# Raw tokens multiplied by centred weights, with a turned copy of the input in memory, in a three-layer attention and routing kernel

## The reference

```python
def layernorm(x):  # (x - mean) / sqrt(var + 1e-5), over the 512 features
    ...
def ffn(x, w_router, w_block):            # x: (8, 1024, 512)
    scores = einsum('bld,d->bl', x, w_router)
    _, top_idx = top_k(scores, 768)       # three quarters of the tokens of a sequence
    processed = gelu(einsum('bkd,de->bke', selected, w_block))
    return x.at[batch_idx, top_idx].set(processed)
x = x + 0.5 * ffn(layernorm(x), ...)
x = x + attention(layernorm(x), ...)      # Wq, latent K and V, softmax, v_up, Wout
x = x + 0.5 * ffn(layernorm(x), ...)
```

## Time and profile before

| | us |
|---|---|
| runs (3), median | 2382.53 |
| lowest, highest | 2381.05, 2382.56 |
| the profiled execution | 2386.42 |
| its span, first to last instruction | 2384.7 |
| PE busy | 2201.2 (92%) |
| DVE busy | 1805.1 (76%) |
| ACT busy | 1176.3 (49%) |
| POOL busy | 404.6 (17%) |
| mean granted TensorE clock | 0.975 |

### The profile page before, as it was taken

One profiled execution on the slowest core, in us unless ns is written; L12 is line 12 of the kernel. 1 busy time (PEld: TensorE's weight loads), 2 busy tenths in 40 slices (PEclk: granted clock), 3 DMA queues, 4 the chain that ended last, 5 costly groups with the idle time before them and its releaser, 6 DMA issues.

```text
span 2384.7 us, 53143 instructions
## 1 busy us (share of the span) xinstructions
PE 2201.2 (92%) x21504; PEld 1338.9 (56%) x21504; DVE 1805.1 (76%) x5077; ACT 1176.3 (49%) x2070; POOL 404.6 (17%) x510
## 2 busy tenths in 40 slices
PE   5789999999999999999998999989998999999997
PEld 4544477445674456744566446754466544765455
DVE  7668767887669877788777886788767888678747
ACT  4245643556435564345644565345643557435552
POOL 2001111212102121021210212111111111121131
PEclk9889999999999999999999999999999999999999
DMA  3200021200302002020020201211021110212000
GB/s 137 106 2 2 2 83 60 72 2 2 106 36 72 3 19 89 37 72 3 19 89 36 73 2 40 68 54 55 2 71 36 70 40 2 71 36 72 2 2 36
DMA packets 69633, 106.42 MB, mean 45 GB/s; under 512 B 2576, under 2 KB 32784, under 8 KB 67344
## 3 DMA queue, kind: packets, MB, share of 16 engines
q1 hardware_dynamic: 69392, 103.03, 12.6%
HBM read 64.75 MB, written 37.75 MB: 43 GB/s over the span
## 4 chain that ended last, share of the span: by engine, by line
PE 75%; DVE 13%; ACT 6%; issue 5%; POOL 1%; DMA 0%; DVEq 0%; POOLq 0%; ACTq 0%
PE psum L829 29%; PE psum L842 17%; PE psum L950 10%; PE psum L957 9%; PE psum L845 5%; ACT pr L809 3%; DVE part L1093 3%; PE psum L871 2%; PE psum L856 2%; DVE psum L1095 2%; DVE junk L1043 1%; DVE nt_l L1018 1%; DVE junk L1028 1%; DVE junk L1045 1%; ACT nt_h L723 1%
## 5 line engine op out<-in xcount | busy, mean ns | idle before, releaser
L809 ACT ACTIVATE pr<-psum 128x512 f32<-128x512 f32 x1152 | 617.7, 597 | 537.8 <-PE psum L845 537.7
L842 PE MATMUL psum<-qk,qk 32*128 32x512 f32 (+3 forms) x4608 | 516.7, 371 | 63.6 <-DVE part L1093 26.9
L1095 DVE CUSTOM_DVE_ANT_0 psum<-psum,mask_b 128x512 f32<-128x512 f32 (+3 forms) x1024 | 473.1, 522 | 106.1 <-PE psum L856 104.7
L842 PEld LDWEIGHTS psum<-qk,qk 32*128 32x128 f32 x4608 | 318.6, 187 | 386.3 <-ACT pr L809 313.9
L856 PE MATMUL psum<-qk,qk 32*128 32x512 f32 (+3 forms) x4608 | 513.1, 371 | 20.6 <-DVE part L1093 19.1
L1093 DVE TENSOR_REDUCE part<-psum 128x1 f32<-128x512 f32 x512 | 325.4, 682 | 58.5 <-PE psum L856 56.5
L856 PEld LDWEIGHTS psum<-qk,qk 32*128 32x128 f32 x4608 | 312.0, 187 | 45.5 <-DVE part L1093 22.8
L950 PE MATMUL psum<-pr,v_sb 128*32 128x512 f32 (+3 forms) x3072 | 314.3, 504 | 1.6 <-ACT ht L723 1.6
L957 PE MATMUL psum<-pr,ones 128*32 128x512 f32 (+3 forms) x3072 | 308.8, 496 | 0.0
L715 POOL TENSOR_SCALAR_AFFINE_SELECT pr<-pr 128x512 f32<-128x512 f32 x256 | 161.6, 650 | 835.2 <-ACT pr L809 835.2
L744 ACT ACTIVATE norm<-x,nmr,rstd 128x512 f32<-128x512 f32 x192 | 153.3, 816 | 163.0 <-DVE nmr L1012 163.0
(11 more groups left out here) (109 smaller groups left out, 3239.1 us busy)
## 6 DMA issues: line engine op xcount, KB each, us to landing
x<-x_dram SPq DMA_DIRECT2D x16, 1024.0 KB, 7.1
spill_x<-x SPq DMA_DIRECT2D x16, 1024.0 KB, 4.8
x<-spill_x SPq DMA_DIRECT2D x16, 1024.0 KB, 7.2
out_dram<-x SPq DMA_DIRECT2D x14, 1024.0 KB, 5.1
w_h<-scratch_o SPq DMA_DIRECT2D x28, 256.0 KB, 3.1
w_l<-scratch_o SPq DMA_DIRECT2D x28, 256.0 KB, 3.3
w_h<-scratch_q SPq DMA_DIRECT2D x6, 1024.0 KB, 4.9
w_l<-scratch_q SPq DMA_DIRECT2D x6, 1024.0 KB, 6.9
```

The costliest lines, as they stand in the source:

```text
L809: nc.scalar.activation(pr_of(b, g, u)[:, 2 * p + place, :], bank(e, place), ACT.Exp, scale=SCALE).then_inc(exp_ready, 1)
L842: eng.matmul(o, (k_h, k_h, k_l)[t][own, P * j:P * (j + 1)], (q_h, q_l, q_h)[t][own, queries], start=(t == 0 and at == 0), stop=False, skip ...
L1095: m = nc.vector.tensor_tensor_reduce(scores, scores, mask_b[:, BANK - w:BANK], 1.0, FAR, ALU.add, ALU.max, top_of)
```

## The change

Routed layers multiply the raw token by a weight from which each column's mean over the 512 inputs is taken, and scale behind the product: ((x - mean) * rstd) @ W = rstd * (x @ (W - column means of W)). The scale is given to the gelu's ACTIVATE as a per-partition operand.

- `WC` (new, once, in the opening): four float32 matmuls of ones by `raw_b` give the column sums, four DVE steps subtract them from `raw_b`. `WS` 0 waits for it.
- Layernorm 0: `NO` and `T` are gone. A second input, `x_turned`, holds x with features on partitions. `XQ` (new) loads it in two DMAs of 1 MB for a sequence, from SP's queue, at the head of group 2 of the sequence before, into the place of `nt_l`. `XH` (new, eight for a sequence, every second chunk of group 2): ACT copies to `nt_h`, POOL subtracts in place to `nt_l`.
- Layernorm 2: `NO` is gone; `T` turns x itself as soon as `O` has been added. ACT's and DVE's parts of `T` stay. Layernorm 1 keeps `NO` and `T`.
- The order of `opening`, `back` and `closing` is rewritten around this. In `opening` WC, four XH and WS 0 stand ahead of the statistics, and the DMAs are ordered turned half, w_block, x, x, router weights, turned half, other weights.
- `G` waits for `rstd`; `GX` no longer waits for `NO`, and in layer 1 for `T` instead.

```diff
     def opening():
-        out = []
+        out = [("WC", 0)] + sum([raw(0, i) for i in range(TC)], []) + [("WS", 0)]
         for c in range(NC):
             for i in range(TC * c, TC * (c + 1)):
                 out += stats(0, 0, i)
             out += scales(0, 0, c)
-        out += [("NO", 0, 0, 0), ("NO", 0, 0, 1)]
-        for i in range(NT):
-            out += [("T", 0, 0, i)] + ([("NO", 0, 0, i + 2)] if i + 2 < NT else []) + dot(0, 0, i)
-            out += [("WS", 0)] if i == TC else [("SC", 0, 0, 0)] if i == 5 else []
-        out += [("SC", 0, 0, 1)]
         for i in range(TC):
-            out += layer(0, 0, i) + [("RT", 0, 0, 2 * i), ("RT", 0, 0, 2 * i + 1)]
-            out += [("WS", 1), ("WS", 2), ("WS", 3)] if i == 1 else []
-        out += [("RF", 0, 0)] + [("GX", 0, 0, i) for i in range(NT)]
-        out += layer(0, 0, 4) + layer(0, 0, 5) + summed(0, 0) + summed(0, 1)
-        out += layer(0, 0, 6) + summed(0, 2) + summed(0, 3) + scales(1, 0, 0) + [("WS", 4)] + layer(0, 0, 7)
+        out += sum([raw(0, i) for i in range(TC, NT)], [])
+            out += dot(0, 0, i)
+        out += layer(0, 0, 0) + layer(0, 0, 1)
+        for i in range(TC, NT):
+            out += dot(0, 0, i)
+        out += [("SC", 0, 0, 0)] + layer(0, 0, 2) + [("SC", 0, 0, 1)] + [("RT", 0, 0, i) for i in range(3)] + [("WS", 1)]
+        out += [("RT", 0, 0, i) for i in range(3, 6)] + layer(0, 0, 3) + [("WS", 2)] + [("RT", 0, 0, 6), ("RT", 0, 0, 7)]
+        out += [("RF", 0, 0)] + [("GX", 0, 0, i) for i in range(NT)] + [("WS", 3)] + layer(0, 0, 4) + layer(0, 0, 5)
+        out += layer(0, 0, 6) + layer(0, 0, 7)
+        out += summed(0, 0) + summed(0, 1) + summed(0, 2) + summed(0, 3) + scales(1, 0, 0) + [("WS", 4)]
...
     def back(b):
-            return [("T", 2, b, i)] + ([("NO", 2, b, i + 2)] if i + 2 < NT else [])
+            return [("T", 2, b, i)]
-        out = added(0) + added(1) + more(maxima, 5) + added(2) + added(3) + scales(2, b, 0)
-        out += added(4) + [("NO", 2, b, 0), ("NO", 2, b, 1)] + more(maxima, 6) + added(5) + turn(0)
-        out += added(6) + more(gathered, 1) + turn(1) + added(7) + more(gathered, 0) + more(turned, 1)
-        out += [("VA", 2, b, 1), ("RS", 2, b, 1)] + turn(2)[:1] + dot(1, b, 0) + [("NM", 2, b, 1)] + more(turned, 0)
+        out = added(0) + added(1) + turn(0) + more(maxima, 5) + added(2) + turn(1) + added(3) + turn(2)
+        out += scales(2, b, 0) + added(4) + turn(3) + more(maxima, 6) + added(5) + turn(4) + dot(1, b, 0)
+        out += added(6) + turn(5) + more(gathered, 1) + dot(1, b, 1) + added(7) + turn(6) + more(gathered, 0) + more(turned, 1)
         out += ([("W2", b + 2, "q", 0)] if b + 2 < B else [])
-        out += layer(1, b, 0) + turn(3)[:1] + [("NO", 2, b, 4), ("NO", 2, b, 5)] + dot(1, b, 1) + dot(1, b, 2)
-        out += layer(1, b, 1) + turn(4) + dot(1, b, 3) + turn(5) + dot(1, b, 4) + turn(6) + [("SC", 1, b, 0)] + turn(7) + dot(1, b, 5)
-        out += layer(1, b, 2) + dot(1, b, 6) + dot(1, b, 7) + layer(1, b, 3) + [("SC", 1, b, 1)]
+        out += scales(2, b, 1) + layer(1, b, 0) + turn(7) + more(turned, 0) + dot(1, b, 2) + dot(1, b, 3) + dot(1, b, 4)
+        out += layer(1, b, 1) + [("SC", 1, b, 0)] + dot(1, b, 5) + dot(1, b, 6)
+        out += layer(1, b, 2) + dot(1, b, 7) + layer(1, b, 3) + [("SC", 1, b, 1)]
...
     def closing(b, left):
-        for i in range(TC, NT):
-            out += added(i)
-        out += scales(2, b, 1) + [("NO", 2, b, 4), ("NO", 2, b, 5)] + added(0) + added(1) + turn(4)
-        out += added(2) + turn(5) + dot(1, b, 4) + added(3) + turn(6) + dot(1, b, 5) + scales(2, b, 0) + turn(7) + dot(1, b, 6)
-        out += dot(1, b, 7) + [("NO", 2, b, 0), ("NO", 2, b, 1)] + layer(1, b, 4) + [("SC", 1, b, 1)]
-        out += dot(1, b, 0) + dot(1, b, 1) + dot(1, b, 2) + dot(1, b, 3) + turn(0)
-        out += turn(1) + layer(1, b, 5) + [("SC", 1, b, 0)] + turn(2) + turn(3)
+        out += added(4) + added(5) + turn(4) + added(6) + turn(5) + added(7) + turn(6) + scales(2, b, 1) + added(0) + turn(7)
+        out += dot(1, b, 4) + added(1) + turn(0) + dot(1, b, 5) + added(2) + turn(1) + dot(1, b, 6) + dot(1, b, 7)
+        out += added(3) + turn(2) + scales(2, b, 0) + [("SC", 1, b, 1)] + dot(1, b, 0) + dot(1, b, 1) + dot(1, b, 2)
+        out += dot(1, b, 3) + layer(1, b, 4) + turn(3) + [("SC", 1, b, 0)] + layer(1, b, 5)
...
-            groups[2] += [[("NO", 0, b + 1, 0), ("NO", 0, b + 1, 1)]]
+            groups[2][0] += [("XQ", b + 1, c) for c in range(NC)]
+            for i in range(NT):
+                groups[2][2 * i + 2] += raw(b + 1, i)
             chunks = groups[3]
-            for u in range(NT):
-                chunks[2 * u] += [("T", 0, b + 1, u)]
-                chunks[2 * u + 1] += [("NO", 0, b + 1, u + 2)] if u + 2 < NT else []
...
+                elif k == "XQ":          # SP
+                    b, c = e[1:]
+                    if b:
+                        sp.wait_ge(s_done, nth["S", b - 1, 1, UNITS - 1, 1])
+                    eng.dma_start(nt_raw[(b + 2) % 3][:, TC * c:TC * (c + 1), :, :], x_turned[b, :, TC * c:TC * (c + 1), :, :]
+                                  ).then_inc(xt_in[c], 16)
...
+                elif k == "XH":          # POOL
+                    pool.wait_ge(xh_ready, nth[e])
+                    nc.gpsimd.tensor_tensor(nt_l[n][:, i, :, :], nt_raw[n][:, i, :, :], nt_h[n][:, i, :, :].bitcast(F32),
+                                            ALU.subtract).then_inc(xl_ready, 1)
...
+                elif k == "XH":          # ACT
+                    act.wait_ge(xt_in[i // TC], 16 * (b + 1))
+                    copy(nt_h[n][:, i, :, :], nt_raw[n][:, i, :, :]).then_inc(xh_ready, 1)
...
+                    act.wait_ge(rstd_ready, nth["RS", 2 * f, b, i // TC])
-                         ACT.Gelu_apprx_tanh).then_inc(gelu_ready, 1)
+                         ACT.Gelu_apprx_tanh, scale=rstd[:, 2 * f, i:i + 1]).then_inc(gelu_ready, 1)
...
+                if k == "WC":            # PE
+                    pe.wait_ge(raw_in[0], 16)
+                    for n in range(NK):
+                        m = eng.matmul(bank(e), ones[:, 0:1].broadcast_to([P, P]), raw_b[:, n, :], start=(n == 0), stop=(n == NK - 1))
+                    m.then_inc(wc_done, 1)
...
+                if k == "WC":            # DVE
+                    dve.wait_ge(wc_done, 1)
+                    for n in range(NK):
+                        nc.vector.scalar_tensor_tensor(out=raw_b[:, n, :], in0=bank(e), scalar=-1.0 / E, in1=raw_b[:, n, :],
+                                                       op0=ALU.mult, op1=ALU.add).then_inc(centered, 1)
```

More of the change, by code:

```diff
@@ L289, in ending @@
         return out
-    sched = [("XL", 0, 0), ("XL", 0, 1)] + opening()
+    sched = [("XQ", 0, 0), ("XL", 0, 0), ("XL", 0, 1), ("XQ", 0, 1)] + opening()
     for b in range(B):
@@ L335, in program_order, with macaron @@
     return sched, beside
-def macaron(nc, x, w_q, w_lat, w_qk, w_vu, w_out, w_router, w_block, scratch_q, scratch_o, spill_x, out):
+def macaron(nc, x, x_turned, w_q, w_lat, w_qk, w_vu, w_out, w_router, w_block, scratch_q, scratch_o, spill_x, out):
     sched, beside = program_order()
@@ L352, in macaron @@
             load_nth[e] = 1 + sum(1 for o in load_nth if o[2] == e[2])
+    norms = [e for e in sched if e[0] == "NO"]
     steps = [e[1:4] for e in sched if e[0] == "S" and e[4] == 0]
@@ L410, in macaron @@
             continue
-        if k == "XT" and e[2] > 0 or k in ("T", "SC", "F") and e[1] == 0 and e[2] > 0 and (k != "F" or e[3] < 2):
+        if k == "XT" and e[2] > 0 or k in ("SC", "F") and e[1] == 0 and e[2] > 0 and (k != "F" or e[3] < 2):
             banks[e] = from_queue(1)
@@ L474, in macaron @@
         nt_l = [over(f"nt{n}_l", region[n] + 16384, [P, NT, NK, P], F32R) for n in range(3)]
+        nt_raw = [over(f"nt{n}_raw", region[n] + 16384, [P, NT, NK, P]) for n in range(3)]
         nt_act = [over(f"nt{n}_act", region[n], [P, NT, NK, P]) for n in range(3)]
@@ L523, in macaron @@
         t_done, th_ready, tl_ready = sem("t_done"), sem("th_ready"), sem("tl_ready")
+        xt_in, xh_ready, xl_ready = [sem(f"xt_in{c}") for c in range(NC)], sem("xh_ready"), sem("xl_ready")
+        wc_done, centered = sem("wc_done"), sem("centered")
         sc_done, srow_ready, scol_ready = sem("sc_done"), sem("srow_ready"), sem("scol_ready")
@@ L865, in _ @@
                     pe.wait_ge(*freed(*user))
-                if k == "T":
-                    s, b, i = e[1:]
-                    pe.wait_ge(no_ready, nth["NO", s, b, i])
-                    slot = nth["NO", s, b, i] % 2
+                if k == "WC":
[3 more added lines that the diff above has]
+                    m.then_inc(wc_done, 1)
+                elif k == "T":
+                    s, b, i = e[1:]
+                    if s == 1:
+                        pe.wait_ge(no_ready, nth["NO", s, b, i])
+                        tile = norm[:, nth["NO", s, b, i] % 2, :]
+                    else:
```

(9 more changed lines are left out.)

28 lines of the change are left out of this document (22 added, 6 removed).

## The result

The changed kernel takes 2327.53 us (median of 4 runs, 2326.72 to 2328.94) against 2382.55 us (4 runs, 2381.05 to 2382.6): 55.0 us less, ratio 0.977, 95% interval 0.9756 to 0.9784. The forecast was 2328, so what has to be examined is whether the terms are right or only their sum.

A forecast was written before the change was run, and what follows sets the result against it. PE was taken as the bound (92% busy, 97% in group 3), DVE's chain at both ends. Terms -42 + 3.5 - 17 - 6.6 + 8 = -54 us took 2382.5 to 2328 us, range 2311 to 2352.

The forecast's parts named there:

- Group 3, -6.0 us a sequence: Group 3, seven times: layernorm 0's eight transposes and waits for `scol` go, 6.0 us a sequence, -42 us in all.
- The unknown: Group 3: whether PE closes the gaps around a removed T; 0.5 us for a T if not, 0.69 us expected.
- Group 2, +0.5 us a sequence: Group 2, seven times: ACT's copies and POOL's subtractions added there cost 0.5 us a sequence, +3.5 in all.
- rival 4: Groups 0 and 3 and opening: other waits shorten too, opening loses only 4 us; 2312 us, chance 0.10.
- The load is hidden by about 4 us: Group 2: turned loads land 4.9 us after issue, wanted 9 us after; cost 0, each us beyond stops ACT one.
- `back`, -2.4 us: `back`, seven times: PE's waits for DVE go as T no longer waits for `norm`; -2.4 us each, -17 in all.
- Gelu with a scale, 0: Gelu on ACT, 128 times: the scale operand adds 0 to 0.22 us each, hidden; cost 0 on the path.
- The closing, -6.6 us: Closing: a shorter chain from last add lets the ranks begin at about 2350.1 instead of 2356.73 us; -6.6 us.
- The opening, +8 us: Opening: weight preparation ahead of the statistics delays the first CB by 7 us, plus 1 for contention; +8 us.
- The term for contention: Opening: DVE's dots beside POOL's last four subtractions are slowed, 1 us added.
- the estimate of 3 us: Opening: by the skill's shared SBUF interface rule, dots beside POOL are delayed, costing some 3 us instead of 1.
- rival 1: `back`: new waits replace the old, PE waits as much as before, only -37 is left; 2345 us, chance 0.15.

The follow-up runs named there:

- run 3: Changed kernel plus 32 unread transposes a sequence on TensorE in group 3, in two blocks of 16, sequences 0 to 6: 2349.84 us, +22.3 us against the changed kernel.
- Run 1: Changed kernel with layernorm 0 of sequences 1 to 7 taken back to normalized, transposed tokens: 2372.54 us, +45.0 us against the changed kernel.
- run 5: Changed kernel with the turned loads of sequences 1 to 7 issued about 9.6 us later: 2382.71 us, +55.2 us against the changed kernel.
- run 2: Changed kernel with layernorm 2 taken back, old `back` and `closing`, second gelu without scale: 2346.3 us, +18.8 us against the changed kernel.
- run 7: Changed kernel with the splits of tiles 4 to 7 of sequence 0 put ahead of the opening's statistics: 2326.25 us.
- run 8: Changed kernel with the opening's statistics ahead of the column sums' subtraction and its dots right behind that: 2321.63 us, -5.9 us against the changed kernel.

## Why the prediction was right

1. **Group 3, -6.0 us a sequence.** Right, and by its own mechanism: the loop takes 23.57 us (23.5 forecast), and each four transposes put back alone cost 0.68 us (0.69 forecast). In the traces the stretch from first to last `S` gives 6.36 us a sequence: 5.5 for eight T, as forecast, and 0.87 for the waits, of which the forecast took 0.5. The unknown, whether neighbours would close up below 0.5 us, is answered by run 3: only if the transposes stood in one block would four cost 0.44.
2. **Group 2, +0.5 us a sequence.** Mis-sized, near the lower bound: the trace shows 0.1 us. Run 1 gives 45.0 us where 42 - 3.5 = 38.5 was the forecast for groups 2 and 3 together. Of the difference of 6.5 us this term has 2.6 and the waits of group 3 have 2.6. Groups 0 and 1 were not in the sum: they are 4.6 us shorter in seven sequences (3.7 with group 2), which is the direction of rival 4; by which wait isn't shown.
3. **The load is hidden by about 4 us.** Right: ACT never waits for it in group 2. The first `XH` needs only the first of the two loads, and in all seven sequences that one lands 4.9 to 5.1 us after issue (4.9 forecast), so some 4 us of the 9 are left. The second lands later and is wanted later. The price outside the cover was too mildly put. The forecast had one us lost for one us late; run 5 shows 7.9 us for a stop of 6. By that the change is worth nothing once ACT's stop reaches 6 us instead of 7.7, that is with a landing 15 us after issue instead of 17.
4. **`back`, -2.4 us.** 2.0 measured in `back` 3, 2.2 as the mean of seven stretches of `project` and `back`: the `scol` wait grew from 0.3 to 0.7, since the dots were not quite done in time.
5. **Gelu with a scale, 0.** Right: 0.69 us for each instead of 0.60, and no wait behind it. The Trainium skill's 93 ns for a pointer operand (ScalarE: Activation LUTs, section "What ACT_TABLE_LOAD costs") agrees: 688 less 598 ns is 90.
6. **The closing, -6.6 us.** From last add to ranks it is 7.1 us, but that is not what the closing gains. The forecast left the last add where it was and so put nothing for the four more `T` ahead of it on PE; they make it 2.3 us later. 4.8 us are gained by the trace, from the first add to the ranks as from the last `S` to the end. With `back`, 15.1 + 4.8 = 19.9 us; run 2 shows 18.8 at the median, 23.6 was forecast.
7. **The opening, +8 us.** The end is right, +8.9 us at the first `S` and +8.8 by subtraction, but the way there isn't. The first CB is 10.7 us later, not 7 and one for contention, and 1.8 of it are made up before the first `S`. The term for contention was 1 us and measured 3.9 (1.05 for `nmr`, 1.07, 0.87 and 0.87 for three dots). Here the rule of the Trainium skill that was set against it (GPSIMD Engine Reference, section "Key points") was the better guide: the estimate of 3 us made by it lies nearer to 3.9 than 1 does. How much of the 3.9 us reaches the end no run shows: run 7 had the dots at full speed, but its statistics began 2.3 us later.

The sum with what was measured: -45.0 - 18.8 + 8.8 = -55.0, where the last term is by subtraction and the sum therefore comes out in any case; forecast -38.5 - 23.6 + 8 = -54. The check on it is the table: it has +8.9 for that term without any subtraction. The mechanisms of the forecast hold, but that it came within 1 us is in part luck: a gain taken 6.5 us too small stood against one taken 4.8 us too large. Rival 4 had that direction for groups 0 to 3, rival 1 the opposite one for `back`; neither is large enough to have decided.

## What to carry to other kernels

Where an engine is 96% busy, the price of an operation there is best read as the difference between two instances of the same loop, one with it and one without; a block of the same instructions alone is cheaper (0.44 against 0.69 us here) and misleads. What replaces it goes where the other engines have slack by the window, and the place matters more than the amount: the same eight splits cost 0.1 us a sequence in one group and 5.3 in the next. Ends of a kernel have their own bound: list what the chain there needs first, put only that first, and price each added preparation against it (a better order of the same work brought the first `S` 10.4 us forward here). Where an operation moves ahead of another, the other moves back: price both, as the closing shows.

## What the runs showed of the hardware

- **VectorE beside GpSimd.** Beside POOL's 128x512 subtraction of two SBUF tiles, DVE steps with two SBUF operands went from 0.75 to between 1.57 and 1.82 us for 128x512, and even one of 128x4 elements from 0.16 to 1.21 us, so it is a delay of 0.8 to 1.1 us for each instruction more than a factor. Not every step is hit as hard: with the splits in group 3 one dot took 1.12 us, and with the statistics first one dot beside POOL's four took 0.73 us. Four steps with an operand in PSUM were not slowed (the column sums' subtraction took 2.47 us for the four beside POOL, in run 8, and 2.48 alone).
- **TensorE's clock after a short stop.** PE stood 6.1 us in a stretch that otherwise ran at a granted clock of 1.00, the 2.4 GHz level. In the 4 us behind the stop the granted clock was 0.50, the 1.2 GHz level, then 0.99, and the first matmuls behind it took 0.79 instead of 0.50 us. The run lost 7.9 us a sequence for a stop of 6.1.
